# Attention slots of a decoder layer on one core: scores, values and transposes as one block, and where the output's split stands

## The reference

```
x = layernorm(x + attn(x))     # causal, within each sequence, 16 heads of 64
x = layernorm(x + xattn(x, c)) # its mask leaves each query one key, so it is a linear map of c
x = layernorm(x + ffn(x))      # 8 experts, the best 2 a token, and a shared one

logits = einsum('bqhd,bkhd->bhqk', q, k) / 8 ; where(causal, -1e5, logits)
attn   = einsum('bhqk,bkhd->bqhd', softmax(logits), v)
out    = einsum('bqhd,hdm->bqm', attn, O_w) + O_b
```

## Time and profile before

| | us |
|---|---|
| median of 3 runs | 476.01 (475.89 to 477.33) |
| the profiled execution, its own time | 476.58 |
| its span in the profile | 474.8 |
| TensorE busy in the span | 449.9 (95%) |
| DVE, ACT, POOL busy | 309.2, 289.4, 206.5 |

### The profile page before, as it was taken

The page is one execution under the profiler, slowest core; times in us unless marked ns, Lnnn a source line. Parts: engine busy times, 40 slices in busy tenths (PEclk is TensorE's granted clock), DMA queues, the critical chain, the costliest instruction groups (busy, mean ns, idle before and its releaser), DMA issues.

```text
span 474.8 us, 11231 instructions
## 1 busy us (share of the span) xinstructions
PE 449.9 (95%) x3645; PEld 396.3 (83%) x3645; DVE 309.2 (65%) x1247; ACT 289.4 (61%) x916; POOL 206.5 (43%) x227
## 2 busy tenths in 40 slices
PE   8999999999999999999999999988997989999981
PEld 6888787988989879888888897978886979999961
DVE  4376796678767656695675768687985343333495
ACT  3686646675576755667557565673543454665565
POOL 1998493530204011211085344744415764655531
PEclk9999999999999999999999999989999899999998
DMA  6830121300400000020021232120132652433765
GB/s 199 308 129 3 59 90 46 135 1 1 135 2 1 1 12 35 24 68 1 0 68 46 79 94 74 46 57 35 44 80 91 168 147 90 118 118 113 241 238 187
DMA packets 26542, 40.16 MB, mean 85 GB/s; under 512 B 3199, under 2 KB 17683, under 8 KB 26483
## 3 DMA queue, kind: packets, MB, share of 16 engines
q1 hardware_dynamic: 21532, 27.86, 19.3%
q0 software_dynamic: 3408, 9.33, 5.5%
q10 hardware_dynamic: 1547, 2.27, 1.5%
HBM read 26.83 MB, written 12.61 MB: 83 GB/s over the span
## 4 chain that ended last, share of the span: by engine, by line
PE 79%; DVE 11%; ACT 4%; issue 3%; DMA 2%; another core or an unknown queue 1%; POOL 0%; ACTq 0%; SPq 0%; POOLq 0%; DVEq 0%
PE bank L300 18%; PE bank L302 17%; PE bank L301 16%; PE bank L811 7%; PE bank L849 6%; PE bank L822 5%; DVE probs L1394 2%; PE bank L990 2%; ACT probs L1151 2%; PE bank L1004 2%; PE bank L980 1%; PE bank L898 1%; DVE probs L1384 1%; DVE xt_lo L1353 1%; DVE xacc L1763 1%
## 5 line engine op out<-in xcount | busy, mean ns | idle before, releaser
L1151 ACT ACTIVATE probs<-probs,negmax 128x128 f32<-128x128 f32 x256 | 99.7, 394 | 49.9 <-DVE negmax L1384 49.8
L300 PE MATMUL bank<-w_hi,ot_hi 128*128 (+1 forms) x284 | 83.3, 293 | 0.7 <-ACT qkv L1122 0.6
L301 PE MATMUL bank<-w_lo,ot_hi 128*128 (+1 forms) x284 | 80.9, 285 | 0.0
L302 PE MATMUL bank<-w_hi,ot_lo 128*128 (+1 forms) x284 | 80.4, 283 | 0.0
L1384 DVE CUSTOM_DVE_ANT_0 probs<-bank,mask 128x128 f32<-128x128 f32 x256 | 61.3, 285 | 12.1 <-PE bank L811 11.9
L596 POOL DMA_INDIRECT xg_dram<-xacc,place x32 | 32.4, 1013 | 81.3 <-PE bank L849 35.6
L300 PE MATMUL bank<-xt_hi,w_hi 128*128 128x512 f32 x144 | 61.5, 427 | 1.3 <-ACT qkv L1114 1.1
L1394 DVE TENSOR_TENSOR probs<-probs,rsum 128x512 f32<-128x512 f32 x64 | 57.3, 896 | 2.2
L1114 ACT ACTIVATE qkv<-bank,cols 128x512 f32<-128x512 f32 x64 | 42.1, 679 | 26.5 <-PE bank L302 26.4
L300 PEld LDWEIGHTS bank<-w_hi,ot_hi 128*128 128x128 f32 x284 | 54.4, 192 | 3.9 <-issue 2.4
L302 PE MATMUL bank<-xt_hi,w_lo 128*128 128x512 f32 x144 | 56.9, 395 | 0.0
(11 more groups left out here) (230 smaller groups left out, 1053.5 us busy)
## 6 DMA issues: line engine op xcount, KB each, us to landing
qkv<-xg_dram SPq DMA_DIRECT2D x39, 128.5 KB
ex_raw<-in_w_experts SPq DMA_DIRECT2D x18, 256.0 KB
w_raw<-in_w_quads SPq DMA_DIRECT2D x10, 256.0 KB, 4.1
xacc<-in_x SPq DMA_DIRECT2D x4, 512.0 KB, 3.6
ex_raw<-in_w_cross SPq DMA_DIRECT2D x4, 512.0 KB, 3.3
w_raw<-in_ctx_t_in ACTq DMA_DIRECT2D x4, 512.0 KB
w_raw<-in_w_quads SPq DMA_DIRECT2D x3, 512.0 KB, 6.1
xacc<-in_x_t SPq DMA_DIRECT2D x3, 512.0 KB, 5.6
```

What stands on the lines that cost most here:

```text
L300: pe.matmul(o, a_hi, b_hi, start=first, stop=False)
L301: pe.matmul(o, a_hi, b_lo, start=False, stop=False)
L302: return pe.matmul(o, a_lo, b_hi, start=False, stop=last)
L1151: nc.scalar.activation(tile, tile, ACT.Exp, scale=-1.0, bias=negmax[:, s.par, h, j:j + 1], accum_out=sums[:, s.par, h, j:j + 1]).then_inc( ...
```

## The change

On TensorE the values of pair p - 2 (last but one) now stand in slot p, right behind the scores, and both `turn`s behind them; all fills follow. So slot 1 has no values, and those of pair 31, the last, stand between the halves of `cross(3, ·)`. They wait for `pt_a`, `pt_b` of the slot before and `ot_ready` of two before. ACT takes the output's hi part behind `exps(0)` (in the last slots, without projections, at the front as before), and `take(1)` stands ahead of `exps(1)` in all slots. DVE takes the lo part behind both masks, in slots 30 and 31 between them, in 32 and 33 at the front. Slot 31 leaves `pt_a` to DVE again. POOL's sends wait for other counts.

```diff
-                s.act_turns = SLOTS - 2 <= p <= SLOTS
+                s.act_turns = p in (SLOTS - 2, SLOTS)
...
                 pool.wait_ge(transposed, 2 * p - 1)
                 send(g, 2 * r)
-                pool.wait_ge(pv_done, p)
+                if p % 2 == 0:
+                    pool.wait_ge(proj_qk, 4 * (p // 2 + 1) + 2)
+                else:
+                    pool.wait_ge(proj_v, 2 * (p // 2 + 1) + 2)
                 send(g, 2 * r + 1)
...
             send(2, 0)
-            pool.wait_ge(pv_done, SLOTS - 1)
+            pool.wait_ge(proj_o, 2 * UNITS - 3)
             send(2, 1)
             split_expert(16)
             send(2, 2)
-            pool.wait_ge(pv_done, SLOTS)
+            pool.wait_ge(pv_done, SLOTS - 1)
             send(2, 3)
...
                     score()
+                if 2 <= s.p <= SLOTS:
+                    values(s)
                 if s.back:
                     turn(0)
+                    turn(1)
                 fill(0)
-                if s.back:
-                    turn(1)
                 fill(1)
                 for then in mid.get(s.p, ()):
                     then()
                 fill(2)
-                if s.back:
-                    pe.wait_ge(pt_a, s.n(1, 0))
-                    pe.wait_ge(pt_b, s.n(1, 0))
-                    pe.wait_ge(v_ready, s.u(2, 2 if s.pp == 1 else 0))
-                    if s.p >= 2:
-                        pe.wait_ge(ot_ready, s.n(1, -1))
-                    vb = vv[s.ub if s.pp == 1 else 1 - s.ub]
...
                 fill(3)
+            def values(s):
+                pe.wait_ge(pt_a, s.n(1, -1))
+                pe.wait_ge(pt_b, s.n(1, -1))
+                pe.wait_ge(v_ready, s.u(2, 0))
+                if s.p >= 3:
+                    pe.wait_ge(ot_ready, s.n(1, -2))
+                vb = vv[1 - s.ub]
+                for j in range(GT):
+                    for h in range(2):
+                        c = s.pp * P + h * DH
+                        mm = pe.matmul(pv_bank[slices(h, DH), slices(j, P)], vb[:, j, c:c + DH],
+                                       probs_t[:, h, slices(j, P)], start=True, stop=True)
+                mm.then_inc(pv_done, 1)
...
-            behind[SLOTS] = [lambda: cross(G - 1, 0), lambda: cross(G - 1, 1)]
+            behind[SLOTS] = [lambda: cross(G - 1, 0), lambda: values(Slot(SLOTS + 1)), lambda: cross(G - 1, 1)]
...
+                if s.evac_o and not s.proj:
+                    take_o_hi()
...
                 if s.front:
                     exps(0)
+                if s.evac_o and s.proj:
+                    take_o_hi()
                 take(0)
                 if s.back and not s.act_turns:
                     take_pt_b()
-                values_first = s.p in mid or s.p in (0, 3, 5)
-                if values_first:
-                    take(1)
+                take(1)
                 for then in mid.get(s.p, ()):
                     then()
                 if s.front:
                     exps(1)
-                if not values_first:
-                    take(1)
...
+                if s.evac_o and not s.front:
+                    take_o_lo()
                 if s.front:
                     mask_and_max(0)
+                if s.evac_o and s.front and not s.proj:
+                    take_o_lo()
+                if s.front:
                     mask_and_max(1)
+                if s.evac_o and s.proj:
+                    take_o_lo()
```

More of the change, by code:

```diff
@@ L837, in slot @@
                 fill(2)
-                if s.back:
-                    pe.wait_ge(pt_a, s.n(1, 0))
-                    pe.wait_ge(pt_b, s.n(1, 0))
-                    pe.wait_ge(v_ready, s.u(2, 2 if s.pp == 1 else 0))
-                    if s.p >= 2:
-                        pe.wait_ge(ot_ready, s.n(1, -1))
-                    vb = vv[s.ub if s.pp == 1 else 1 - s.ub]
[L846 to L851, removed]
-                fill(3)
+                fill(3)
+            def values(s):
[11 more added lines that the diff above has]
+                mm.then_inc(pv_done, 1)
             def cross(g, half):
@@ L1156, in take_pt_b, with take_o_hi @@
                     nc.scalar.activation(probs_t[:, 1, :], tr_bank[1][:, :], ACT.Copy).then_inc(pt_b, 1)
-                if s.evac_o:
+                def take_o_hi():
                     act.wait_ge(pv_done, s.n(1, -1))
@@ L1405, in add_o, with take_o_lo @@
                                             ALU.add).then_inc(o_added, 1)
-                if s.evac_o:
+                def take_o_lo():
                     dve.wait_ge(ot_hi_ready, s.n(1, -1))
```

## The result

| | before | after |
|---|---|---|
| median, 5 runs each on one chip | 476.47 us (475.89 to 477.33) | 486.41 us (485.15 to 490.89) |
| ratio | | 1.0223, 95% interval 1.0179 to 1.0268 |
| the profiled execution, its span | 476.58, 474.8 | 490.89, 489.1 |
| TensorE busy in the span | 449.9 (95%) | 451.9 (92%) |
| DVE, ACT, POOL busy | 309.2, 289.4, 206.5 | 317.2, 292.8, 206.0 |

The kernel became 9.9 us slower, where 472.2 us and 3.8 us faster were forecast. The profiled execution of after is the slowest of its five, 4.5 above their median.

A forecast was written before the change was run, and what follows sets the result against it. TensorE's order was taken to bound slots 8 to 30, but not the end. The terms -5.6 - 1.0 + 0.5 - 0.6 + 3.05 = -3.65 us gave a 472.4 us median, stated as 472.2, range 467.3 to 476.2.

The forecast's parts named there:

- Values behind the scores, 0.20 us a slot: Slots 2 to 29: 28 groups of values, each 0.20 us cheaper right behind the scores, -5.6 us.
- the first rival: By data type: scores and values share full f32 and pay nothing between them, 0.34 us a slot, 468.3 us; 12%.
- the second rival: Second transposes: TensorE waits at turn(1) for a late normalise(1) in some 12 middle slots, +9.6 us, 482; 12%.
- these two terms: Slot 1 loses its group of values, -1.0 us; slot 2's turn(1) waits for a later normalise(1), +0.5 us.
- I cost all that at nothing: Slots 2 to 29: the later work on ACT, DVE and POOL stays hidden, 0 us, two exceptions aside.
- the wait of slot 5 stays: Slot 5: DVE is held by one normalise of 4.35 us whose end doesn't move; 0, at best -1.4 us.
- The end, +3.05: Slots 30 to 33: TensorE is not the bound there and the change adds 3.05 us in four steps.
- slot 30, `chosen` behind the lo part: Slot 30: take_o_lo goes between the masks, ahead of `chosen`, for which rank() waits, +0.65 us.
- slots 31, 32 to cross(3, 0): Slots 31 and 32: counts wait behind a longer chain, clock fall likelier than not, +0.7 us (-0.4 to +1.1).
- values between the halves of cross: Near the end: the group that left slot 1 stands between the halves of cross, +1.2 us.
- what follows: Slot 33: take_o_lo and list_early() come later, ahead of add_o(0), in a chain to the last x2_turn, +0.5 us.
- The third rival: The end takes all the gain back, by an earlier clock fall or a chain 3 us longer, 475.4 us; 14%.

The follow-up runs named there:

- experiment 3: The changed kernel with take(1) and exps(1) on ScalarE back in the old order: 498.55 us, ratio 1.0486 to before.
- experiment 1: The changed kernel with POOL's bias rows of experts and cross attention left out, two memsets instead: 475.96 us, ratio 0.9995 to before.
- experiment 5: The changed kernel with POOL's complete bias-row work cut into pieces of at most 512 columns: 475.43 us, ratio 0.9982 to before.
- experiment 7: The changed kernel with slot 30's lo part behind both masks, and DVE's counts and lists ahead of it in slots 32 and 33: 481.72 us, ratio 1.0132.
- experiment 8: The changed kernel with DVE's order in the last slots repaired in part and POOL's bias rows in pieces: 474.34 us, ratio 0.9968 to before.
- experiment 9: The new order only in slots 1 to 29, last slots as before, POOL's bias rows in pieces: 471.61 us, ratio 0.9874 to before.
- experiment 10: The new order only in slots 8 to 29, first and last slots and POOL as before: 473.66 us, ratio 0.9932 to before.
- with pieces: The changed kernel with POOL's bias-row work cut into pieces of at most 512 columns: 475.43 us; with DVE's last slots partly repaired as well: 474.34 us.
- experiment 4: The kernel before with take(1) ahead of exps(1) in all slots and nothing else of the change: 476.69 us, ratio 1.0016.
- experiment 2: The kernel before with POOL's bias rows of experts and cross attention left out, two memsets instead: 474.86 us, ratio 0.9968.
- experiment 6: The kernel before with POOL's complete bias-row work cut into pieces of at most 512 columns: 474.29 us, ratio 0.997.

## Why the prediction was wrong

**Values behind the scores, 0.20 us a slot: right**, a little high. Even slots give 0.20, odd 0.15; over the 22 middle slots -3.2 in place of -4.4 and the -0.4 or so of vanished waits. In slot 23 such a wait is gone (-0.53 in all), in slots 12 and 28 new ones came: x2_turn(·, 1), which follows the second fill, now waits 0.3 us for DVE's norm, and fill(2) of slot 28 waits 0.4 us as before, where I had let the wait go. By data type (0.34, the first rival) is refuted: the group takes 1.03, not 0.88. The Trainium skill's rule of modes (page "TensorEngine Tiling (Array Packing)", "Tiling Modes") fits, with three changes a slot for four; it gives no price and does not speak of data types, so the 0.20 and the odd slots' 0.15 are this case's.

**Second transposes: not the cause.** In the middle slots TensorE never waits for normalise(1); all its waits for L1398 are two, 2.8 us, in slots 1 and 2. There the second rival's wait came true once, but by way of POOL. Slot 1 should have lost its group (-1.0): in the five other profiles with this order in slots 1 and 2, and in that of experiment 3, it did (4.94 for 5.97), in after it did not. Slot 2 should have taken 0.5 more: it took 0.5 more in experiments 1 and 5, 1.1 to 1.3 in 7 to 9 and 2.0 in after. So these two terms, -0.5 together, came out at -0.6 to +0.2, and at +2.0 in after's profiled execution alone.

**"I cost all that at nothing" and "the wait of slot 5 stays ... its end does not move with TensorE (0, at best -1.4)": this is the step that failed**, by 6.5 us in slot 5 (and, with POOL's weight splits, by 2.5 in slots 1 and 2 of this one execution, 0.7 at most in the others). I had the row of 4.35 us and read it as a fixed event of DVE. It was a collision whose size is set by which DVE operation starts behind which POOL operation. The new order moved normalise(0) of slot 4 from 3.69 us into its slot to 5.25, at the place where POOL starts. The row of POOL stood beside it in the trace; I didn't put the two together. Experiments 1 and 5 remove slot 5's loss by touching POOL alone, 10 by leaving the old order alone in slots 0 to 7.

The twelve profiles show it without exception. Of the operations of 128x512 whose two inputs are both in SBUF (normalise, split and their like), 227 start while a `tensor_tensor` or cast of POOL runs, and none ends less than 0.54 us behind POOL's end; 699 start while POOL runs nothing, and none takes over 0.70 us. What the rows show is what the Trainium skill says on the page "SBUF — State Buffer", section "Who interferes with whom": a DVE instruction with two SBUF inputs and a GpSimd instruction that reads SBUF contend for the shared port pair, and whichever starts first keeps it for the whole instruction. The trace agrees: normalise and the split have two SBUF inputs, the masks (one from PSUM) aren't held, nor is normalise beside a memset; and POOL is held in turn (in experiment 7 its cast of 128x1024 at 22.70, which starts while a normalise runs, takes 1.50 us for the usual 1.04). One row goes beyond the two inputs: the cast of 128x8 below has a single one and was held too.

**The end, +3.05: the mechanism right, the sizes too small**, 5.39 in all:

| step | forecast | after | without the clock's part or with pieces |
|---|---|---|---|
| slot 30, `chosen` behind the lo part | +0.65 | +1.20 | +1.21 with pieces; +0.83 with the lo part behind the masks as well |
| slots 31, 32 to cross(3, 0) | +0.7 | +1.18 | +1.00 with pieces |
| values between the halves of cross | +1.2 | +2.49 | +1.12 at full clock (experiment 1) |
| what follows | +0.5 | +0.52 | |

Slot 30's second half is again DVE's small pieces behind POOL: the cast of 128x8 took 0.90 us for 0.17, the next 1.24 for 0.51, while the last one got 0.9 cheaper. The fall of the clock in slot 31, "likelier than not", is in all six profiles that have the block in the last slots (the scores of slot 31 take 1.88 to 2.08 us). But I had set the sum against a before in which it falls too, and that was the odd one: of the six profiles with the old end it is the only one, the others take 1.16 us for these scores and 40.0 to 40.2 for the whole end, where before took 41.46. Against that end the block's costs 5.2 to 6.8 us, or 4.3 to 4.6 after the repair of experiments 7 and 8. Why the clock spares the old order is not shown. The third rival (the end takes it all back) was therefore right about the end and missed the start.

Ahead of the fall, or while it came, TensorE stood still for 2.6 to 3.0 us in one piece, waiting for `chosen`; in the old end it is twice 0.8 to 1.0 us.

The Trainium skill's remark that a transpose doesn't count as activity as a matmul does (page "TensorE: Matmul & The Clock Gate", Part 4) was not tested apart from that: no run here changed the transposes alone.

**What stays open.** Of after's five runs only the profiled one shows that it met POOL in slot 5; the profiled ones of experiments 3 and 7 met it too. Why odd slots save 0.15 and not 0.20 isn't tried.

## What to carry to other kernels

An operation whose duration in the trace is several times its usual one is not a constant: look at what the other engines did at its start, and treat it as a collision that a shift of a microsecond can remove or multiply. Long POOL operations beside a DVE on which the critical path rests are to be cut into short ones; here that is worth 1.4 us even to the old kernel (474.29 beside 475.72) and 11 to the new. A reordering that pays where TensorE is the bound should end before the stretch where it isn't: the same change with the old order in slots 30 to 33, and POOL's work in pieces, gives 471.6 us, 1.3% under the kernel before.

## What the hardware showed that I had not expected

- DVE's operations with two SBUF inputs that follow one another are caught by one POOL operation after the other: 5.03, 2.60 and 6.14 us against POOL's 4.60, 2.67 and 5.98, so that DVE moves at POOL's pace for 14 us.
- Two executions of the same instructions differ by 1.8 us in slots 1 and 2 (16.97 us in after, 15.20 in experiment 7), with POOL's weight splits 0.9 us earlier and the first scores 0.8 us later in the longer one.
- The same order of work in slots 30 and 31 met a clock that fell in before (scores of slot 31: 2.08 us, from 313.40) and none in experiment 4 (1.16 us, from 314.02) nor in 2, 6, 9 and 10, which arrive 2 to 4 us earlier. One profile of a kernel doesn't tell whether the clock falls at a given place.
